# First attention of a four-layer block: GpSimd multiplies the sums of a pair of heads by the inverses of the row sums

## What is computed

```
q = _qdq(x) @ _qdq(wq).T + bq                 # 16 heads of 32 channels
k, v = jnp.split(cond @ wkv.T + bkv, 2, axis=-1)
attn = jax.nn.softmax(jnp.einsum('bnhd,bmhd->bhnm', q, k) * scale, axis=-1)
o = jnp.einsum('bhnm,bmhd->bnhd', attn, v).reshape(B, N, C)
out = _qdq(o) @ _qdq(wp).T + bp
```

## Time and profile before

| | us |
|---|---|
| median of 3 runs (3143.09 to 3145.14) | 3145.06 |
| the profiled execution | 3140.41 |
| its span in the trace | 3138.7 |
| first attention, in the trace | about 167 to 545 |
| VectorE busy over the span | 2332.1 (74%) |
| TensorE busy | 2921.9 (93%) |
| ScalarE busy | 2088.6 (67%) |
| GpSimd busy | 1394.8 (44%) |

### The profile page before, as it was taken

How to read it: one execution, slowest core, us unless ns; L and a number is a source line. 1 busy time by engine, 2 the same in 40 slices (tenths; PEclk the granted TensorE clock), 3 DMA queues, 4 the chain that set the end, 5 groups by cost and what they waited for, 6 DMA issues and landing times. The chain is left out here.

```text
span 3138.7 us, 56425 instructions
## 1 busy us (share of the span) xinstructions
PE 2921.9 (93%) x15383; PEld 2362.9 (75%) x15414; DVE 2332.1 (74%) x4699; ACT 2088.6 (67%) x4262; POOL 1394.8 (44%) x1761
## 2 busy tenths in 40 slices
PE   6878998887999999989999899999999999899988
PEld 4656666675888877778888688888888888688845
DVE  5679998864777658766676189999898898734377
ACT  4468987421666646556666488888888888633366
POOL 4412000404000056267777377777777777442132
PEclk9989999898999999999999999999999999999999
DMA  6896664206888777546455523323322322195510
GB/s 202 267 234 163 159 153 107 88 31 215 274 284 264 221 238 242 155 135 180 141 171 178 181 68 99 99 72 97 99 74 95 99 75 95 38 323 179 176 39 35
DMA packets 401824, 474.32 MB, mean 151 GB/s; under 512 B 52276, under 2 KB 267220, under 8 KB 401652
## 3 DMA queue, kind: packets, MB, share of 16 engines
q1 hardware_dynamic: 388692, 419.72, 44.4%
q0 software_dynamic: 12960, 52.61, 4.8%
HBM read 304.30 MB, written 167.92 MB: 150 GB/s over the span
## 5 line engine op out<-in xcount | busy, mean ns | idle before, releaser
L2861 POOL TENSOR_SCALAR h_probs<-h_exp,h_rowsum_inv 128x512 f32<-128x512 f32 x512 | 356.9, 697 | 278.1 <-PE h_pT L2709 261.5
L2789 DVE TENSOR_REDUCE h_neg_max<-h_scores 128x1 f32<-128x512 f32 x512 | 349.3, 682 | 143.7 <-PE h_scores L2701 143.5
L2751 ACT ACTIVATE h_exp<-h_scores,h_neg_max 128x512 f32<-128x512 f32 x512 | 356.0, 695 | 110.2 <-DVE h_neg_max L2789 101.0
L2802 DVE TENSOR_TENSOR h_probsT_lo<-h_pT,h_probsT_hi 128x512 fp32r<-128x512 f32 x512 | 348.3, 680 | 0.0
L2709 PEld LDWEIGHTS h_pT<-ident,h_probs 128*128 128x128 f32 x2048 | 255.0, 140 | 71.5 <-POOL h_probs L2861 2.3
L2709 PE MATMUL h_pT<-ident,h_probs 128*128 128x128 f32 x2048 | 307.1, 272 | 0.9 <-POOL h_probs L2861 0.8
L2760 ACT CAST h_probsT_hi<-h_pT 128x512 fp32r<-128x512 f32 x512 | 301.1, 588 | 0.9 <-PE h_pT L2709 0.9
L2977 PE MATMUL k_acc<-k_w_hi,k_cat 128*128 128x512 f32 x512 | 200.5, 392 | 12.3 <-POOL k_w_lo L3058 11.4
L2724 PE MATMUL h_pO<-h_probsT_hi,n_lo 128*128 128x512 f32 x512 | 203.3, 397 | 0.0
L2978 PE MATMUL k_acc<-k_w_lo,k_cat 128*128 128x512 f32 x512 | 199.9, 390 | 0.0
L910 ACT ACTIVATE b_probs<-b_scores,b_neg_max 128x512 f32<-128x512 f32 x256 | 179.7, 702 | 25.2 <-DVE b_neg_max L937 25.2
(11 more groups left out here) (460 smaller groups left out, 9033.0 us busy)
## 6 DMA issues: line engine op xcount, KB each, us to landing
e_w_raw<-in_w SPq DMA_DIRECT2D x24, 1792.0 KB, 7.8
lnT<-g_out SPq DMA_DIRECT2D x160, 256.0 KB, 2.3
n_raw<-lnT SPq DMA_DIRECT2D x64, 512.0 KB, 5.2
e_w_raw<-in_w SPq DMA_DIRECT2D x24, 896.0 KB, 9.8
n_raw<-lnT SPq DMA_DIRECT2D x64, 256.0 KB, 5.1
n_raw<-v SPq DMA_DIRECT2D x64, 256.0 KB, 5.7
cat<-h_cat SPq DMA_DIRECT2D x128, 128.0 KB, 1.8
k_cat<-cat SPq DMA_DIRECT2D x128, 128.0 KB, 5.1
```

The lines of the kernel that those rows point to most:

```text
L2751: nc.scalar.activation(Pr[:, r % 4], pS[r % 2][:], ACT.Exp, bias=nmax[:, r % 4:r % 4 + 1], accum_out=rsum[:, r % 4:r % 4 + 1]).then_inc(ex ...
L2789: v.tensor_reduce(nmax[:, r % 4:r % 4 + 1], pS[r % 2][:], axis=AX, op=ALU.max, negate=True).then_inc(nmax_done.sem, 1)
L2802: v.tensor_tensor(PTl[:, br * HPG + h, :, bass.ts(q, P)], pT[r % 4][:], PTh[:, br * HPG + h, :, bass.ts(q, P)], ALU.subtract).then_inc(lo_ ...
L2861: nc.gpsimd.tensor_scalar(Pn[:, r % 4], Pr[:, r % 4], rinv[:, r % 4:r % 4 + 1], 1.0, ALU.mult, ALU.mult).then_inc(norm_done.sem, 1)
```

## The change

`normalise` on VectorE becomes `sum_parts`: it forms the inverses and the sum, without waiting for itself, and counts both in a new semaphore `summed`, two for each pair. The multiply moves to GpSimd as `scale_pair`, which waits for `summed`, and for the first pair of a group for the store that last read the output buffer, and counts `o_done` as before. GpSimd does the two pairs of group k-1 at the head of its work for group k, and the last two at the end. TensorE's transposes into `b_pR` now wait for `summed` of the pair before, instead of `o_done`.

```
@@ l0_attention
-        dve_link = m.sem("dve_link")
...
-        oT_done, oTr_done, o_done = m.flag("oT"), m.flag("oTr"), m.flag("o_done", depth=4)
+        oT_done, oTr_done, summed, o_done = m.flag("oT"), m.flag("oTr"), m.flag("summed", 2), m.flag("o_done", depth=4)
@@ gpsimd
+            def scale_pair(np):
+
+                gb, pair = np // PAIRS % 2, np % PAIRS
+                pool.wait_ge(summed.sem, summed.done(np))
+                if pair == 0:
+                    pool.wait_ge(o_out[gb], 16 + np // (2 * PAIRS) * 16)
+                nc.gpsimd.tensor_tensor(O[:, gb, :, 2 * pair * DH0:2 * (pair + 1) * DH0].rearrange("p k (h c) -> p k h c", h=2),
+                                        osum[:, np % 2],
+                                        rinv[:, np % 2].rearrange("p h k -> p k h").unsqueeze(3).to_broadcast([P, QT, 2, DH0]),
+                                        ALU.mult).then_inc(o_done.sem, 1)
+
             for k in range(NG):
+                for pair in range(PAIRS):
+                    if k >= 1:
+                        scale_pair((k - 1) * PAIRS + pair)
                 pool.wait_ge(s_done.sem, s_done.depth + max(k * UN, UN // 2))
...
+            for pair in range(PAIRS):
+                scale_pair((NG - 1) * PAIRS + pair)
             pool.wait_ge(folded, 2)
@@ tensor, o_transposes
-                pe.wait_ge(o_done.sem, o_done.past(np, 1))
+                pe.wait_ge(summed.sem, summed.past(np, 1))
@@ vector
-            def normalise(i, r):
+            def sum_parts(i, r):
...
-                link = Links(dve, dve_link, np, 2)
                 dve.wait_ge(o_done.sem, o_done.free(np))
-                link(nc.vector.reciprocal(rinv[:, pb], rsum[:, head:head + 2]))
+                nc.vector.reciprocal(rinv[:, pair_buffer(r)], rsum[:, head:head + 2]).then_inc(summed.sem, 1)
                 dve.wait_ge(oTr_done.sem, oTr_done.done(np))
-                link(nc.vector.tensor_reduce(osum[:, pb], pR[:].rearrange("p k (h w c) -> p k h c w", h=2, w=2),
-                                             axis=AX, op=ALU.add))
-                if h == 1:
-                    dve.wait_ge(o_out[gb], 16 + i * 16)
-                nc.vector.tensor_tensor(O[:, gb, :, (h - 1) * DH0:(h + 1) * DH0].rearrange("p k (h c) -> p k h c", h=2), osum[:, pb],
-                                        rinv[:, pb].rearrange("p h k -> p k h").unsqueeze(3).to_broadcast([P, QT, 2, DH0]),
-                                        ALU.mult).then_inc(o_done.sem, 1)
-                link.end()
-
-            pipeline(dve, N, 2 * UN, [(low, 4), (maxima, 0), (normalise, 10)])
+                nc.vector.tensor_reduce(osum[:, pair_buffer(r)], pR[:].rearrange("p k (h w c) -> p k h c w", h=2, w=2),
+                                        axis=AX, op=ALU.add).then_inc(summed.sem, 1)
+
+            pipeline(dve, N, 2 * UN, [(low, 4), (maxima, 0), (sum_parts, 10)])
```

More of the change, by code:

```diff
@@ L952, in normalise @@
                 gb, h, q = place(r)
-                pb, head = pair_buffer(r), gb * HG0 + h - 1
-                link = Links(dve, dve_link, np, 2)
+                head = gb * HG0 + h - 1
                 dve.wait_ge(o_done.sem, o_done.free(np))
-                link(nc.vector.reciprocal(rinv[:, pb], rsum[:, head:head + 2]))
+                nc.vector.reciprocal(rinv[:, pair_buffer(r)], rsum[:, head:head + 2]).then_inc(summed.sem, 1)
                 dve.wait_ge(oTr_done.sem, oTr_done.done(np))
-                link(nc.vector.tensor_reduce(osum[:, pb], pR[:].rearrange("p k (h w c) -> p k h c w", h=2, w=2),
-                                             axis=AX, op=ALU.add))
-                if h == 1:
-                    dve.wait_ge(o_out[gb], 16 + i * 16)
-                nc.vector.tensor_tensor(O[:, gb, :, (h - 1) * DH0:(h + 1) * DH0].rearrange("p k (h c) -> p k h c", h=2), osum[:, pb],
-                                        rinv[:, pb].rearrange("p h k -> p k h").unsqueeze(3).to_broadcast([P, QT, 2, DH0]),
-                                        ALU.mult).then_inc(o_done.sem, 1)
-                link.end()
-            pipeline(dve, N, 2 * UN, [(low, 4), (maxima, 0), (normalise, 10)])
+                nc.vector.tensor_reduce(osum[:, pair_buffer(r)], pR[:].rearrange("p k (h w c) -> p k h c w", h=2, w=2),
+                                        axis=AX, op=ALU.add).then_inc(summed.sem, 1)
+            pipeline(dve, N, 2 * UN, [(low, 4), (maxima, 0), (sum_parts, 10)])
 E0, HID, TOPK = 8, 448, 2
```

## The result

The changed kernel takes 3123.08 us (median of 4 runs, 3117.15 to 3125.14); the kernel before, on the same chip, 3145.10 (4 runs). The ratio is 0.9927 with an interval of 0.991 to 0.9943, so the gain is 22 us. The forecast was 3127.8 with a range that ended at 3124.0: the direction is right, the gain of 17.3 us is too small, and the median lies 0.9 us outside the range. A second set of runs of the same kernel (the first experiment) gave 3122.98 against 3143.27, so this is not one lucky set.

What follows compares the result with a forecast made beforehand. VectorE, 95% busy, was taken to bound the first attention; -17.7 us at its pair ends and +0.4 at the stage's end make -17.3, from the median 3145.06 to 3127.8 us, range 3124.0 to 3136.5.

Steps and rivals of the forecast that it cites:

- What VectorE gives back behind the sum: First attention, 31 pair ends: sum to next low half falls from 36.6 to 18.9 us in all, 17.7 us gained.
- The branch: VectorE's loop branch at six pair ends: needs 0.51 us, hidden under the sum's 0.61; at most 1.0 us if it shows.
- The wait ahead of the sum stays: VectorE between inverse and sum: the sum waits for TensorE's transposes anyway, so 0 gained, far bound 1.0 us.
- the inverse's link: VectorE's wait for its own inverse before the sum: removing it taken as 0, at most 5 x 0.19 = 1.0 us.
- Do the others follow?: ScalarE and TensorE at pair ends: they keep up, so VectorE's 0.46 us per pair is real; four pairs in 43.1 us.
- The replay: Pair end at 345.64 replayed: maximum 0.46 us earlier, ScalarE 0.07 us late, caught up two to three units later.
- The end of the stage: Last pair's multiply on GpSimd: ends at about 544.06 instead of 543.70, 0.4 us later, charged in full.
- ScalarE becomes the bound: Rival: only ScalarE's 9.3 us of waiting for VectorE can be taken up; gain 8.9 us, 3136.2 us; chance 0.10.
- The own wait is free: Rival: VectorE's wait on its own semaphore costs nothing, the sum itself takes 0.73 us; 3.7 us less gain, 3131.5; chance 0.07.
- The transfers crowd: Rival: later constant and weight loads delay a stack of keys, one stall of 1 to 4 us; 3128.8 to 3131.8; chance 0.08.
- The shared interface: Slower rival: GpSimd's multiplies hold up VectorE's low halves or maxima, 23.7 us lost, 3151.5 us; chance 0.03.

Runs made afterwards that it cites:

- the first experiment: The changed kernel run once more, unaltered, beside the kernel before: 3122.98 us (5 runs) against 3143.27 (11 runs), ratio 0.9937.

## Why the prediction was too small, step by step

**What VectorE gives back behind the sum**, forecast 36.6 - 18.9 = 17.7 us. Measured 17.72. (At the six branches the trace of before reads 1.24 twice, 1.25 three times and 1.29 once, not 1.25 once; the sum is the same.) The branch, left as an open 1.0 us, is hidden (0.61 at 400.10), and the kernel with the sum's link measures what it would cost uncovered: 0.54 us, against the forecast's 0.51.

**"The wait ahead of the sum stays"**, priced at 0 with a far bound of 1.0 us. *This is the step that failed*: it gave 3.6 us (3.85 by the changed kernel's second profile). 2.3 of them are the inverse's link, 1.0 the form of TensorE's wait. They also fit pair end by pair end: 0.24, 0.41, 0.24 and 0.91 us with 0.07 for the link at each and 0.09 and 0.06 for TensorE's wait at the second and third give 0.31, 0.57, 0.37 and 0.98, and the kernel before has 0.31, 0.58, 0.37 and 0.99. Of the rest 0.27 us lies at the third pair of the stage (0.64 before instead of 0.37), where the scores had just waited for keys. The error has a shape worth seeing. The forecast argued that the sum waits for TensorE's transposes anyway (0.71 us behind their start), so the link cannot matter. But the bracket names who was waited for last, not in what form the engine waits, and that form changed on both engines. The sum now starts 0.63 us behind the transposes' start:

```profile
367.31 0.60 PE L910 MATMUL b_pR<-ident,b_oT 128*128 128x128 f32 x4
...
367.94 0.69 DVE L972 TENSOR_REDUCE b_o_sum<-b_pR 128x256 f32<-128x512 f32 x1
```

TensorE and VectorE, in order of time. Before, it was 344.93 and 345.64. A constant distance to the releaser (0.71 at every pair) was read as the chip's own delay; 0.08 of it hung on the link, and came back with it.

**"Do the others follow?"** Yes. The pairs' period went from 45.08 to 42.56 us per loop turn, below the 43.1 foreseen, and ScalarE's wait for the maxima, 9.3 us before, no longer shows among the waits; about 1 us was foreseen. The replay found the slack thin, and so it is: with half the work for the maxima there is only 0.5 us more to be had. The gain itself is VectorE's time at the pair ends (17.7 + 3.6 of the 21.4 us). What the replay did not see is how close a second limit lay: with eased maxima the kernel before stops at 336.09 us, and the gain could pass that only because the low half, and with it the transposes and the cast behind it, also comes earlier.

**The end of the stage**, forecast +0.4, measured +1.74. GpSimd's multiply was estimated at 0.74 us and took 0.63, so that part came out cheaper: the last multiply ends 0.24 us later behind the last sum. The rest is 1.5 us: from the end of the last multiply to the next stage it takes 3.33 us instead of 545.53 - 543.70 = 1.83. For an end with GpSimd last no row of before had an instance; it should have carried a bound.

The sum: -17.7 - 3.6 - 0.1 (unassigned) + 1.7 = -19.7 instead of -17.3. Taken from the same 3145.06, that is 3125.4, inside the range; the median came 2.3 us lower still, within the spread of single runs (3117.15 to 3125.14), for which the range's lower end left 1 us. That the two misses in the stage partly cancel, 3.6 us of gain and 1.3 us of loss not foreseen, is luck.

**The rivals.** *ScalarE becomes the bound*: half true. There was such a cap, and easing VectorE by half maxima alone met it at 9.6 us, near the rival's 9.3 us (one run; the likeness may be chance). But this change moved the cap too, since ScalarE's waits for the transposes shrank. These are the waits of the kernel before, 200 to 540 us, and of the changed one, 185 to 525 us:

```profile
ACT b_probsT_hi L919 <- PE b_pT L867: 27.3, 37, 1.5
```

```profile
ACT b_probsT_hi L934 <- PE b_pT L882: 22.8, 38, 1.3
```

An engine's wait for one releaser is no cap on what it can gain when the change also moves its other releasers. *The own wait is free*: refuted; with the sum's wait alone put back it is 0.12 us at each pair end and 7.1 in all with the branch. *The transfers crowd*: refuted for the changed kernel; the crowd was in the old order. *The shared interface*: refuted by 64 extra multiplies.

## What to carry to other kernels

A wait on an engine's own semaphore costs twice: its own 0.07 to 0.12 us, and whatever it uncovers behind it, a loop's branch above all (0.54 us). An added wait can cost even when it is long met, so compare the instructions ahead of an operation and not only whom it waits for. Move the dependent instruction a few steps back first (here half of the gain, on one engine), and to another engine second. Before easing a busy engine further, halve its work in a throwaway kernel: at 97% busy VectorE here had at most 0.5 us left to give, and in the kernel before, at 95%, 9.6.

## What was new about the hardware

- A second wait that is long met still delayed an operation, by 0.07 us at VectorE's sum (0.63 to 0.71 behind the transposes) and, of another form, by 0.1 us at TensorE's product (0.25 to 0.36 and 0.06 to 0.15 behind the copy). In both the wait that ends last stood as an instruction of its own further ahead.
- The loop's branch cost VectorE 0.54 us behind a wait for its own sum (1.26 instead of 0.72) and nothing where only the sum stood ahead of it (0.61) or a multiply whose wait was long met (0.33).
- From the end of the last multiply to the next stage's first operation of VectorE, with the barrier of all engines between, it took 3.3 us when the multiply was GpSimd's and 1.5 to 1.8 when it was VectorE's.
- GpSimd's two-input multiply of 128x256 took 0.63 us, 1.5 times VectorE's 0.43, and did not slow VectorE's maxima or low halves.
